# The score stage of a graph kernel gathers packed tiles into a ring and multiplies them there tile by tile

## The reference

```python
# N = 6250 nodes, E = 206250 edges sorted by dst, 128 features
x = _layernorm(x + L0(x))         # two relational layers
x = _layernorm(x + L1(x))         # an attention layer over the same edges

# L0, twice:
xt = jnp.einsum('nd,rde->rne', x, W)
agg = jax.ops.segment_sum(xt[rel, src], dst, num_segments=x.shape[0])
x = relu(agg + x @ SW + b)

# L1:
q = (x_norm @ Wq + bq).reshape(num_nodes, NH, HD)      # k, v likewise; NH 8, HD 16
scores = jnp.einsum('ehd,ehd->eh', q[src], k[tgt]) / np.sqrt(HD)
scores = scores + (curv @ Wc + bc)                     # curv: 128 features of each edge
smax = jax.ops.segment_max(scores, tgt); p = jnp.exp(scores - smax[tgt])
probs = p / jax.ops.segment_sum(p, tgt)[tgt]
messages = probs[:, :, None] * v[tgt]
out = jnp.zeros_like(x).at[src].add(messages) @ Wo + bo
x = x + out; x = x + relu(layernorm(x) @ W1 + b1) @ W2 + b2
```

## Time and profile before

| | |
|---|---|
| median of 3 timed runs | 8829.8 us (8828.51 to 8844.46) |
| profiled execution, its time | 8832.9 us |
| profiled execution, its span | 8830.7 us |
| PE busy | 6622.3 us, 75% |
| DVE busy | 5953.0 us, 67% |
| ACT busy | 3267.1 us, 37% |
| POOL busy | 6353.0 us, 72% |
| score stage, about 4239 to 6345 us | 2106 us |
| prepare stage | 0 to 134.8 us |

### The profile page before, as it was taken

One profiled execution on the slowest core, in us unless ns is written; L12 is line 12 of the kernel. 1 busy time (PEld: TensorE's weight loads), 2 busy tenths in 40 slices (PEclk: granted clock), 3 DMA queues, 4 the chain that ended last, 5 costly groups with the idle time before them and its releaser, 6 DMA issues. The chain is left out here.

```text
span 8830.7 us, 190462 instructions
## 1 busy us (share of the span) xinstructions
PE 6622.3 (75%) x29670; PEld 5222.0 (59%) x29671; DVE 5953.0 (67%) x18071; ACT 3267.1 (37%) x10181; POOL 6353.0 (72%) x6651
## 2 busy tenths in 40 slices
PE   6566666666788999889788889889655666666667
PEld 4444444444555556555688888888535656655554
DVE  5444444444667777777788888888845666766667
ACT  4233333332222223222455555555433333333322
POOL 4777777776777777777677777777577777777752
PEclk7555555555555555555555555555556777777779
DMA  5222222222222222222455555555435666666653
GB/s 195 60 66 67 66 67 66 66 67 61 55 63 63 63 63 62 62 63 63 119 137 137 138 138 137 137 137 137 105 87 136 152 152 151 156 152 153 154 136 77
DMA packets 1029052, 919.43 MB, mean 104 GB/s; under 512 B 209196, under 2 KB 909799, under 8 KB 1028905
## 3 DMA queue, kind: packets, MB, share of 16 engines
q0 software_dynamic: 211840, 439.50, 18.4%
q1 hardware_dynamic: 627672, 338.49, 15.2%
q10 hardware_dynamic: 189400, 139.98, 7.8%
HBM read 727.42 MB, written 189.28 MB: 104 GB/s over the span
## 5 line engine op out<-in xcount | busy, mean ns | idle before, releaser
L1784 POOL DMA_INDIRECT slots<-big,stage_index x1664 | 1620.9, 974 | 510.8 <-issue 449.8
L1322 POOL DMA_INDIRECT big<-q,stage_index x1664 | 1580.7, 950 | 549.5 <-issue 451.3
L732 POOL DMA_INDIRECT big<-xt,stage_index x1616 | 1524.7, 943 | 540.3 <-issue 454.4
L732 POOL DMA_INDIRECT big<-xt_next,stage_index x1616 | 1525.6, 944 | 524.0 <-issue 476.6
L750 PE MATMUL stage_ps_agg<-stage_hot,stage_msg 128*128 128x128 f32 x6656 | 1619.0, 420 | 253.8 <-ACT stage_msg L711 238.7
L750 PEld LDWEIGHTS stage_ps_agg<-stage_hot,stage_msg 128*128 128x128 f32 x6656 | 1408.5, 312 | 560.3 <-issue 469.3
L782 DVE TENSOR_TENSOR big<-big,stage_ps_agg 128x128 f32 x3328 | 952.6, 286 | 1162.3 <-PE stage_ps_agg L750 797.4
L711 ACT ACTIVATE stage_msg<-big 128x128 f32 x3328 | 755.5, 297 | 2126.1 <-POOLq L721 1470.3
L1821 PE MATMUL stage_ps_val<-nodes_a,big 128*128 x3328 | 660.6, 361 | 665.1 <-ACT big L1747 645.7
L1821 PEld LDWEIGHTS stage_ps_val<-nodes_a,big 128*128 128x128 f32 x3328 | 577.4, 261 | 730.5 <-issue 729.8
L1837 PE MATMUL stage_ps_sums<-stage_hot,big 128*128 128x128 f32 x4160 | 765.2, 348 | 117.5 <-DVE big L1957 111.0
(11 more groups left out here) (363 smaller groups left out, 10412.6 us busy)
## 6 DMA issues: line engine op xcount, KB each, us to landing
big<-slots SPq DMA_DIRECT2D x1976, 66.0 KB
big<-in_edge_attr_dram SPq DMA_DIRECT2D x1664, 64.0 KB
stage_trow<-targets ACTq DMA_DIRECT2D x830, 128.0 KB
big<-q,stage_index POOLq DMA_INDIRECT x1664
slots<-big,stage_index POOLq DMA_INDIRECT x1664
big<-xt,stage_index POOLq DMA_INDIRECT x1616
big<-xt_next,stage_index POOLq DMA_INDIRECT x1616
xt_next<-stage_xo SPq DMA_DIRECT2D x98, 256.0 KB
```

The lines of the kernel that those rows point to most:

```text
L732: pool.indirect_dma_start(self.ring[:, k * D:(k + 1) * D], None, self.xt, bass.IndirectOffsetOnAxis(ap=self.index[:, k:k + 1], axis=0))\
L1322: pool.indirect_dma_start(qrow[q][:, j * D:(j + 1) * D], None, d["q"], bass.IndirectOffsetOnAxis(ap=index[q][:, j:j + 1], axis=0))\
L1784: pool.indirect_dma_start(d["slots"], bass.IndirectOffsetOnAxis(ap=index[q][:, j:j + 1], axis=0), total[q][:, j, :], None).then_inc(s_sc[q ...
```

## The change

The score stage takes over the ring of the layers. What gathers is now a class `Gather` of its own, and `Layer` extends it. In `score` it gathers rows of `d["q"]` into the ring in `big`, 1616 packed tiles instead of 1664, at indices that VectorE makes at the stage's start from the layers' row table (`tile_source`, a shift by three). ScalarE makes indices as in the layers (`make_index`). VectorE loads the four places of a group of pairs and the count of landed groups into its registers and multiplies each pair's 128 columns on its own, at its place in the ring. Score and scatter then work by pairs, so the table of window tiles goes, with its 13 gathers, its 13 matmuls and its copies in `prepare`. What prepare turns at its end (target, row) is turned between steps 17 and 19 instead. The host pads the edges with copies of the first and last one, and the edge features with 128 rows at each end.

```diff
@@ prepare
-        for to, at, ready, landed in ((packed, start_i, START, s_rows_in),
-                                      (packed2, start2_i, PAIR_TABLES, s_rows2_in)):
-            pool.wait_ge(s_v, ready)
+        pool.wait_ge(s_v, PAIR_TABLES)
+        for c in range(KC):
...
-            if k == TILING:
-                pe.wait_ge(s_v, RANKED)
-                nc.tensor.matmul(cnt_ps[0:1, 128:128 + W], wval[:, 2:3], ranked[:, :], start=True, stop=True)
-                for c in range(KC):
-                    done = nc.tensor.matmul(cnt_ps[:, 16 + 3 * c:19 + 3 * c], hot[:, c * P:(c + 1) * P], wval[:, :],
-                                            start=True, stop=True)
...
+            if k == TURN_OLD:
+                pe.wait_ge(s_v, NUMBERED)
+                turn(penalty)
+                turn(source)
+            if k == TURN_TARGET:
+                pe.wait_ge(s_v, TARGETED)
+                turn(target)
+            if k == TURN_ROW:
+                turn_pairs(row)
...
-        pe.wait_ge(s_v, TARGETED)
-        turn(target)
-        pe.wait_ge(s_v, NUMBERED)
-        turn_pairs(row)
@@ score
-    index = slots("index", SLOTS, [P, G], I32)
-    qrow = [room(G * D) for q in range(SLOTS)]
+    tile_source = m.sb("tile_source", [P, K], I32)
+    a = Gather(nc, m, t, d["q"], tile_source, t["big"][:, 0:RING * G * D],
+               None)
...
-        with pool.Fori(0, TURNS) as i:
-            for q in range(SLOTS):
-                g = i * SLOTS + q
-                ring_index(pool, s_index, g + 1, passed)
-                for j in range(G):
-                    pool.indirect_dma_start(qrow[q][:, j * D:(j + 1) * D], None, d["q"],
...
+        a.gather(pool)
...
+            a.make_index(act, x)
...
-            if x.live(3) and x.live(3 - EARLY):
-
-                if x.live(3 - SLOTS):
-                    act.wait_ge(s_freed, x.at(3 - SLOTS) + 1)
-                nc.scalar.activation(index[x.slot(3)][:, :], t["source"][:, bass.ds(x.at(3) * G, G)],
-                                     ACT.Copy).then_inc(s_index, 1)
...
+        v.sem_inc(a.s_freed, SLOTS)
+        for cols in (slice(0, AHEAD * G), slice(AHEAD * G, K)):
+            nc.vector.tensor_scalar(tile_source[:, cols], t["row"][:, cols], R.bit_length() - 1, None,
+                                    ALU.arith_shift_right).then_inc(s_source, 1)
...
             if x.live():
                 h, q = x.slot(0, 2), x.slot()
+                at = offsets(nc, mybir.EngineType.DVE, t["pair_at"], x.at() * G, G, (RING * G - 1) * D)
+                need = v.value_load(t["pair_need"][:, bass.ds(x.at() * G, 1)], min_val=1, max_val=TILE_GROUPS)
                 v.wait_ge(s_k, x.at() + 1)
-                v.wait_ge(s_q[q], x.turn() * (16 * G) + (16 * G + at[q]))
+                ring_index(v, a.s_landed, need, a.passed)
                 if x.live(-1):
                     v.wait_ge(s_qk, x.at(-1) + 1)
-                nc.vector.tensor_tensor(prod, ps_k[h][:, :], qrow[q], ALU.mult).then_inc(s_prod, 1)
+                for j in range(G):
+                    last = nc.vector.tensor_tensor(prod[:, j * D:(j + 1) * D], ps_k[h][:, j * D:(j + 1) * D],
+                                                   a.ring[:, bass.ds(at[j], D)], ALU.mult)
+                last.then_inc(s_prod, 1)
...
                 v.wait_ge(s_prod, x.at() + 1)
+                v.sem_inc(a.s_freed, 1)
...
-
-                v.sem_inc(s_freed, 1)
@@ Gather.gather
                 ring_index(pool, self.s_index, g + 1, self.passed)
                 ring_index(pool, self.s_freed, g + (LAG_GROUPS + 1 + SLOTS - RING), self.passed)
                 for j in range(G):
                     if j == G - 1 and (r or not isinstance(i, int) or i):
                         landed(i, r - 1)
                     k = r * G + j
-                    pool.indirect_dma_start(self.ring[:, k * D:(k + 1) * D], None, self.xt,
+                    pool.indirect_dma_start(self.ring[:, k * D:(k + 1) * D], None, self.rows,
```

More of the change, by code:

```diff
@@ L117, in prepare @@
     smaller, ranked = m.sb("smaller", [W, W]), m.sb("ranked", [W, W])
[L118 to L125, removed]
+    wbase = m.sb("wbase", [W, 1])
+    tile_no, begun_pairs = (region(a)[0:W, :] for a in (5, 3))
     ends_t = m.sb("ends_t", [KC, P, 2])
     packed = t["big"][:, 0:3 * K].bitcast(I32)
-    packed2 = m.sb("packed2", [P, 3 * K], I32)
     pair_hot = t["slot_of"][0:W, :]
-    row, source, target, penalty = (by_tile(region(a)) for a in (3, 4, 5, 6))
+    target, penalty = (by_tile(region(a)) for a in (5, 6))
     valid, key, first, last = (by_tile(region(a)) for a in (7, 8, 3, 4))
@@ L134, in prepare @@
     source = by_tile(t["row"].bitcast(FP32))
-    one_here, one_next = (by_tile(region(a)) for a in (8, 7))
+    row, one_here, one_next = (m.sb(n, [P, KC, P]) for n in ("row", "one_here", "one_next"))
     ends = m.sb("ends", [P, KC, 2])
@@ L287, in order @@
                 pe.wait_ge(s_v, PAIR_HOT)
+                nc.tensor.matmul(cnt_ps[0:1, 128:128 + W], wbase[:, :], ranked[:, :], start=True, stop=True)
                 for c in range(KC):
@@ L380, in _ @@
                 act.wait_ge(s_pe, TURNED)
-                nc.scalar.activation(both_t[:, :], cnt_ps[0:2 * KC, 256:256 + P], ACT.Copy).then_inc(s_turned, 1)
-            if k == PAIR_TURNING:
-                act.wait_ge(s_pe, TURNED2)
-                nc.scalar.activation(both2_t[:, :], cnt_ps[0:2 * KC, 256:256 + P], ACT.Copy).then_inc(s_turned, 1)
+                nc.scalar.activation(tables_t[:, :], cnt_ps[0:3 * KC, 256:256 + P], ACT.Copy).then_inc(s_turned, 1)
+            if k == TURN_OLD:
+                keep("penalty")
+                keep("source")
+            if k == TURN_TARGET:
+                keep("target")
+            if k == TURN_ROW:
+                keep("row")
             if k == LATE:
@@ L389, in _ @@
                     .then_inc(s_turned, 1)
-                keep("penalty")
-                keep("source")
-        keep("target")
-        keep("row")
     @block.vector
@@ L489, in _ @@
             .then_inc(s_v, 1)
-        link(nc.vector.tensor_scalar(penalty, valid, BIG, -BIG, ALU.mult, ALU.add))
-        starts, goes_on = marks[:, :, 0:P + 1], marks[:, :, P + 1:2 * P + 2]
-        own = marks[:, :, 2 * P + 2:MARKS].rearrange("p c (a e) -> p c a e", e=P)
-        link(nc.vector.memset(goes_on, 0.0))
-        by_word = lambda a: a.rearrange("p (c e w) -> p c e w", e=P, w=3)
-        v.wait_ge(s_rows_in, KC * 16)
-        link(nc.vector.tensor_copy(key, by_word(packed)[:, :, :, 1]))
-        link(nc.vector.tensor_copy(source, by_word(packed)[:, :, :, 0]))
         v.wait_ge(s_pe, OF_PAIRS)
@@ new lines, in _ @@
+        starts, goes_on = marks[:, :, 0:P + 1], marks[:, :, P + 1:2 * P + 2]
+        own = marks[:, :, 2 * P + 2:MARKS].rearrange("p c (a e) -> p c a e", e=P)
+        link(nc.vector.memset(goes_on, 0.0))
+        v.wait_ge(s_pool, NEED_CONST)
+        v.wait_ge(s_turned, 1)
+        link(nc.vector.tensor_scalar(at_tile[:, :], tables_t[0:KC, :], RING * G - 1, 7,
+                                     ALU.bitwise_and, ALU.arith_shift_left))
+        link(nc.vector.tensor_scalar(need[:, :, 1], need[:, :, 1], RING * G - 1, None, ALU.bitwise_and))
@@ new lines, in _ @@
+        v.wait_ge(s_rows_in, KC * 16)
+        link(nc.vector.tensor_copy(key, by_word(1)))
+        link(nc.vector.tensor_copy(source, by_word(0)))
+        link(nc.vector.tensor_copy(row[:, :, :], by_word(2)))
+        link(nc.vector.scalar_tensor_tensor(row[:, :, :], source, float(R), row[:, :, :], ALU.mult, ALU.add))
+        nc.vector.tensor_tensor(row[:, :, :], row[:, :, :], valid, ALU.mult).then_inc(s_v, 1)
+        link(nc.vector.tensor_tensor(target, key, over_edges(pair_val[:, :, 4]), ALU.subtract))
```

217 lines of the change are left out of this document (89 added, 128 removed).

## The result

The changed kernel takes 9023.5 us (median of 4 runs, 9021.8 to 9026.8); the kernel before took 8829.2 us beside it. The ratio is 1.0218, 95% interval 1.0201 to 1.0234: slower by 194 us. The forecast was 8985 us (+155). The profiled execution takes 9022.2 us (span 9020.2), against 8832.9 before: +189.3.

What follows compares the result with a forecast made beforehand. VectorE becomes the bound: 4.55 + 0.57 + 0.27 = 5.39 us a group against the gathers' 4.87, +156 us; with +1.5 at the stage's start and -2 in prepare, 8985 us (+1.8%). Range 8890 to 9080.

Steps and rivals of the forecast that it cites:

- What bounds: Score stage before: GpSimd's gathers set 5.02 us a group; VectorE's own group is 4.55 us, with 0.47 us of slack.
- Fewer gathers: Score stage: 1616 gathers for 1664 lower GpSimd's floor by 60 us to 4.87 us a group; VectorE's 165.2 us wait goes.
- Two register loads: VectorE's queue behind the reciprocal: first multiply 1.44 us after the reciprocal's start against 0.87, +0.57 us a group.
- Rival A: Score stage: the loads hide behind the waiting reciprocal, gathers bound the stage, kernel 8770 us; chance 0.09.
- Rival B: A draw: VectorE's group 4.97 to 5.06 us, first multiply 1.02 to 1.11 us behind the reciprocal's start, 8812 to 8847; chance 0.04.
- Rival C: Dearer registers: both VectorE loads take 0.59 us, a group 5.91 us, kernel about 9200 us; chance 0.09.
- Four multiplies: VectorE in score: four 128-wide multiplies for one, 0.215 us apart, with semaphore changes +0.27 us a group.
- Start of the stage: Score stage's start: first gather waits for a shift, first multiply for three gathers of the second group, +1.5 us.
- Prepare: Prepare stage: 13 matmuls go and turning moves earlier, -2 us; index gathers at about 38 us, marks done by 107.
- Layers and scatter: These stages keep their instructions and only table names change: 0 us.

Runs made afterwards that it cites:

- e3: The kernel before, with its 512-wide multiply cut into four of 128: 8820.5 us, ratio 0.9987.
- e4: The kernel before, with two unused loads meant behind the reciprocal; only the one-word load with its assertion was built: 8830.6 us, ratio 0.9998.
- e2: The changed kernel with one 512-wide multiply of a fixed table; the unused four-word load was left out, leaving one load: 8782.6 us, ratio 0.9944.
- e11: The changed kernel with the four-word load behind the previous group's reduction, its register copies behind the last scan, no assertion: 8778.6 us, ratio 0.9940.
- e6: The changed kernel with a second four-word load of the same addresses, used by two of the four multiplies: ratio 1.0384.
- e7: The changed kernel with both loads moved ahead of the reciprocal's wait, behind the copy in front of it: ratio 1.0366.
- e8: The changed kernel with the next group's four-word load behind this group's reduction, register copies behind the reciprocal, no assertion: ratio 0.9966.
- e10: The changed kernel with one 512-wide multiply of a fixed table at a loaded address, both loads kept: 8944 us, ratio 1.0129.
- e1: The changed kernel, VectorE waiting for the tile group of its own number, without the one-word load and its assertion: 8854.8 us, ratio 1.0026.
- e5: The changed kernel with a register maximum in place of the one-word load's assertion, both loads kept: ratio 1.0126.

## Why the prediction held, and where its sizes were off

**What bounds.** Right: GpSimd before, VectorE after. VectorE's own group of 4.55 us is confirmed: the rest of 3.667 and 0.87 make 4.54. e3 and e4 each put something into its 0.47 us of slack and cost nothing. GpSimd's waits for VectorE's release (91.2 us) and for an index (86.7 us) came to 178 us, where over 150 was forecast.

**Fewer gathers.** Right in size, and unused: the floor of 4.87 us a group shows only where VectorE is shorter, 4.908 in e2 and 4.901 in e11. The wait for rows went, as forecast.

**Two register loads, the mis-sized term.** Forecast +0.57 us a group (1.44 from reciprocal to multiply); the trace has 1.588, +0.72; the missing 0.15 are 61 us over 415 groups, and 11 us less in the multiplies and 4 us in VectorE's own group work the other way. Three things were small in what I took over from ScalarE: the one-word load takes 0.339 us and not 0.319 (+0.02), the register operations are 0.07 longer and not 0.03 (+0.04), and the remaining 0.09 lies in what stands between and behind them: the gaps between the queue's entries come to 0.42 us here and to 0.31 on ScalarE, and the semaphore wait takes 0.050 us and not 0.017. The mechanism is as forecast, with two loads on the queue and the first behind the start of the reciprocal, in all groups.

Rival A (the loads hide) gave 8770 us and is refuted by the trace, by e6 and by e7. By the rule of the Trainium skill, Perfetto Trace Analysis, Per-engine timelines, the sequencer is ready for the next instruction once one is pushed into the wait queue, before its semaphores are satisfied. This trace differs: the first register operation of L1188 starts at 5003.7 with the reciprocal (5003.65), and not while the reciprocal waited for the copy, and in no group of the stage is it earlier. The row of L1472 is no single case either. In 408 groups of the kernel before, its register operation starts 0.05 us behind the end of scan L1457, which the instruction in front of it waits for, and ahead of that instruction. The measurement decides.

Rival B said that a draw needs a first multiply 1.02 to 1.11 us behind the reciprocal, with the four multiplies in place. e8 is such a kernel: recip 1.073, a group of 4.968 us, and 0.34% under the kernel before, a little better than the 8812 us that the rival's lower end gives. (e4 has 1.08 us too, but drew for another reason: its own group of 3.67 + 1.08 = 4.75 us stays under the gathers' pace.) Rival C wanted loads of 0.5 us and more; none of the 832 on VectorE's queue in the stage takes more than 0.371 us.

The range had a slip: it was given as a group of 5.17 to 5.61 us, but the bounds that it names add up to 4.55 + 0.40 + 0.20 = 5.15 and 4.55 + 0.76 + 0.40 = 5.71. The measured 5.491 lies in both.

**Four multiplies.** Forecast +0.27 us; the rest grew by 0.243 in the trace; e10 puts the whole part at 0.19, and e3, where the four multiplies stand in the kernel before, likewise (3.855 against 3.667). The spacing is 0.20 us (0.88 - 0.28 = 0.60 for three) where 0.215 was taken, and the reduction starts 1.04 us behind the first multiply (1.03).

**Start of the stage.** Forecast +1.5 us, because the first multiply would wait for three gathers of the second group. It didn't: its wait ends with the keys (PE L1352, 8.2 us), and the landing was passed on at 4246.6, 0.9 us before the multiply. -0.7 instead.

**Prepare.** Forecast -2 us, measured -2.3: the first layer's gathers start at 133.6 us, before at 135.9. The index gathers start at 38.6 (38) and the last mark operation at 107.4 (107). The size is not firm, since programs with the same prepare differ by more: the first layer starts between 133.2 and 136.0 us in the four with the old one, and between 129.1 and 133.6 in the nine with the new one.

**Layers and scatter.** Forecast 0. The score stage starts 5.9 us earlier, 3.6 more than prepare gives. I leave that open, but it is no more than these programs scatter by: e3 and e4 have the layers of the kernel before, and their first score gathers start at 4240.1 and 4243.5 us, against 4245.9; of those with the layers of the changed kernel e1 starts at 4236.6 and e5 at 4248.3.

## What to carry to other kernels

A load of an address into a register is work on the issuing engine's queue. Ask which already issued instruction runs over it: the same four-word load costs its full length behind the reciprocal once the 0.87 us of cover are used up (e6), and nothing behind the reduction (e8); the pair of loads costs more in front of the reciprocal than behind it (e7). Saving work on the engine that sets the pace (60 us of gathers here) gives nothing if the other engine's slack (0.47 us a group) is overdrawn to pay for it: add up both engines' groups. And look in the built program or its trace at whether an added instruction is there, before reading anything from its time.

## What was not expected

The assertion behind a one-word load costs 0.19 us on VectorE's queue, over half as much as the load (e5). Four register copies cost 0.21 us behind the reciprocal and 0.12 behind the scan, where nothing waits for them (e8, e11). The small gaps between queue instructions, and between the last of them and the multiply (34 to 102 ns each, nine of them), make up 0.4 of the 1.59 us.
